# Moving the first norm's gain and shift off VectorE in a two-branch transformer block on one core

## The reference, cut to what matters

```python
# x: 16 x 256 x 128, so 32 tiles of 128 tokens with 128 features each
def _ln(x, g, b, eps=1e-05):
    return (x - mu) / jnp.sqrt(var + eps) * g + b
def _mlp(x, w1, b1, w2, b2):
    return _gelu(x @ w1 + b1) @ w2 + b2
# attention branch, on x already normed once without gain
n = _ln(x, ln_g, ln_b)
W1 = _mlp(n, h1_w1, h1_b1, h1_w2, h1_b2)
W2 = _mlp(n, h2_w1, h2_b1, h2_w2, h2_b2)
W3 = jnp.tril(jnp.einsum('bzn,bsn->bzs', W1, W2))
t = jnp.einsum('bzs,bsm->bzm', W3, n)
t = _ln(_gelu(t), ln_g, ln_b)
out = x + _mlp(_ln(x + t, ln_g, ln_b), fm_w1, fm_b1, fm_w2, fm_b2)
# then a second branch: silu(x w1) * (x w2), two gelu layers of 512 x 512, w3
```

## Time and profile before

| | |
|---|---|
| median of 3 runs | 365.95 us (365.81 to 366.39) |
| span of the profiled execution, first to last instruction | 362.6 us |
| PE, PEld busy | 350.1 us, 289.2 us |
| DVE, ACT, POOL busy | 319.9 us, 305.2 us, 147.2 us |

### The profile page before, as it was taken

One profiled execution on the slowest core, in us unless ns is written; L12 is line 12 of the kernel. 1 busy time (PEld: TensorE's weight loads), 2 busy tenths in 40 slices (PEclk: granted clock), 3 DMA queues, 4 the chain that ended last, 5 costly groups with the idle time before them and its releaser, 6 DMA issues.

```text
span 362.6 us, 6039 instructions
## 1 busy us (share of the span) xinstructions
PE 350.1 (97%) x1788; PEld 289.2 (80%) x1788; DVE 319.9 (88%) x954; ACT 305.2 (84%) x552; POOL 147.2 (41%) x213
## 2 busy tenths in 40 slices
PE   6989999999999999999999999999999999999993
PEld 5867687778888888888888888888888887788992
DVE  5889999999999999889989989998969998886936
ACT  5999999997779979988599888897799569959892
POOL 4168842860546052504750286003920174044411
PEclk9999999999999999999999999999999999999998
DMA  7507020000000000000010001000000001001111
GB/s 233 174 14 245 4 60 1 1 2 1 3 0 0 2 0 2 17 13 2 1 29 3 0 0 33 0 1 2 1 0 2 0 2 31 0 2 29 32 30 33
DMA packets 8804, 9.08 MB, mean 25 GB/s; under 512 B 577, under 2 KB 6722, under 8 KB 8770
## 3 DMA queue, kind: packets, MB, share of 16 engines
q1 hardware_dynamic: 8226, 8.41, 7.7%
q10 hardware_dynamic: 544, 0.26, 0.2%
HBM read 6.57 MB, written 2.10 MB: 24 GB/s over the span
## 4 chain that ended last, share of the span: by engine, by line
PE 67%; ACT 13%; DVE 10%; issue 5%; DMA 2%; POOL 1%; SPq 1%; POOLq 0%; DVEq 0%; ACTq 0%
PE bank L1224 8%; PE bank L1226 8%; PE bank L1240 6%; PE bank L1241 6%; PE bank L1123 4%; PE bank L1104 4%; PE bank L1108 4%; PE bank L1105 4%; PE bank L1120 4%; PE bank L1121 4%; PE bank L1206 4%; PE bank L1209 4%; ACT h_hidden_hi L510 3%; PE bank L1046 2%; ACT bank L515 2%
## 5 line engine op out<-in xcount | busy, mean ns | idle before, releaser
L715 DVE TENSOR_TENSOR ffn_gate_lo<-bank,ffn_gate_hi 128x512 fp32r<-128x512 f32 (+1 forms) x72 | 44.1, 626 | 6.0 <-ACT bank L584 4.9
L510 ACT ACTIVATE h_hidden_hi<-bank,cols 128x512 fp32r<-128x512 f32 x64 | 46.1, 760 | 3.5 <-PE bank L1108 3.2
L515 ACT ACTIVATE bank<-bank,cols 128x512 f32<-128x512 f32 x64 | 45.1, 739 | 0.3
L715 DVE TENSOR_TENSOR h_hidden_lo<-bank,h_hidden_hi 128x512 fp32r<-128x512 f32 x64 | 43.0, 681 | 2.5 <-ACT bank L515 2.5
L584 ACT ACTIVATE bank<-bank,cols 128x512 f32<-128x512 f32 (+1 forms) x72 | 43.7, 620 | 0.7
L1224 PE MATMUL bank<-ffn_gate_hi,ffn_w_hi 128*128 128x512 f32 (+1 forms) x108 | 40.5, 381 | 0.2 <-DVE ffn_gate_lo L715 0.2
L1226 PE MATMUL bank<-ffn_gate_lo,ffn_w_hi 128*128 128x512 f32 (+1 forms) x108 | 39.3, 370 | 0.2 <-DVE ffn_gate_lo L715 0.2
L578 ACT ACTIVATE ffn_h_hi<-bank,cols 128x512 fp32r<-128x512 f32 (+1 forms) x36 | 23.0, 646 | 13.5 <-PE bank L1226 8.3
L578 ACT ACTIVATE ffn_gate_hi<-bank,cols 128x512 fp32r<-128x512 f32 (+1 forms) x36 | 23.2, 647 | 10.6 <-PE bank L1226 8.3
L364 POOL TENSOR_TENSOR XR<-X,ln_x_r 128x512 f32<-128x512 f32 x8 | 8.3, 1042 | 53.6 <-DVE bank L861 53.4
L715 DVE TENSOR_TENSOR ffn_h_lo<-bank,ffn_h_hi 128x512 fp32r<-128x512 f32 (+1 forms) x36 | 22.0, 626 | 8.0 <-ACT bank L584 7.8
(11 more groups left out here) (164 smaller groups left out, 1132.3 us busy)
## 6 DMA issues: line engine op xcount, KB each, us to landing
raw<-ffn_w SPq DMA_DIRECT2D x5, 512.0 KB, 3.9
out<-X SPq DMA_DIRECT2D x7, 256.0 KB, 2.3
raw<-attn_w SPq DMA_DIRECT2D x6, 256.0 KB, 4.9
X<-x SPq DMA_DIRECT2D x3, 256.0 KB, 5.6
raw<-ffn_w SPq DMA_DIRECT2D x1, 256.0 KB, 3.2
X<-x ACTq DMA_DIRECT2D x1, 128.0 KB, 2.5
X<-x SPq DMA_DIRECT2D x1, 128.0 KB, 2.3
out<-X SPq DMA_DIRECT2D x1, 128.0 KB, 1.8
```

What stands on the lines that cost most here:

```text
L510: nc.scalar.activation(dst, bank(f"{L}u{j}", c)[:, :], ACT.Gelu, bias=bias_of(L, j)).then_inc(*hi[L].done(c, j))
L515: nc.scalar.activation(u[:, :], u[:, :], ACT.Gelu, bias=bias_of(L, j)).then_inc(*act2[L].done(c, j))
L715: return nc.vector.tensor_tensor(dst, whole, high.bitcast(f32), ALU.subtract)
```

## The change

The first norm is written without gain and shift by one DVE pass. The up weights of h1 and h2 are scaled by the gain, their biases get the shift times the raw weights, and POOL makes the token form with gain and shift in two passes over NF after PE has transposed it. The bias `fm_b2` is loaded by a DMA with one element per partition. All lists of calls and `TURNS` are laid anew.

```diff
+    UP_PIECES = [PIECE[name] for name in ("h1u", "h2u", "fmu")]
+        h_bias = sb("h_bias", [P, 2 * J])
-        b2_row = M[0:1, 0, :]
@@ SP @@
             attn_piece(2)
-            sp.dma_start(b2_row, rows[2:3, :]).then_inc(b2_in, 16)
             x_piece(1, 1, 2)
             for i in (3, 4, 5):
                 attn_piece(i)
             x_piece(2, 2, 3)
+            sp.dma_start(fm_b2[:, :], rows[2:3, :].rearrange("o d -> d o")).then_inc(b2_in, 16)
             for i in (0, 1):
                 sp.wait_ge(*attn_lo.at(0, 2 * i + 1))
+                if i == 0:
+                    sp.wait_ge(*h_b.at(0))
                 ffn_piece(i)
@@ POOL @@
+            def n_gain(c):
+                if c == 0:
+                    pool.wait_ge(*rows_ready.at(0))
+                pool.wait_ge(*nT.at(c))
+                nc.gpsimd.tensor_tensor(NF[:, :, :], NF[:, :, :], row(R_G), ALU.mult).then_inc(*n_made.done(c, 0))
+
+            def n_shift(c):
+                pool.wait_ge(*n_made.at(c, 0))
+                nc.gpsimd.tensor_tensor(NF[:, :, :], NF[:, :, :], row(R_B), ALU.add).then_inc(*n_made.done(c, 1))
@@ ACT: attn_w_hi @@
-                if i == PIECE["fmu"]:
+                if i in UP_PIECES:
@@ ACT: n_high @@
-                act.wait_ge(*n_v_ready.at(c, T - 1))
+                act.wait_ge(*n_made.at(c, 1))
@@ ACT: bias_of, up_hi (c == 0, j == 0), fm_evict (c == 0) @@
-                return cols[:, C_B1[L] + j:C_B1[L] + j + 1]
+                return h_bias[:, C_B1[L] + j:C_B1[L] + j + 1]
-                        act.wait_ge(cols_in, 16)
+                        act.wait_ge(*h_b_added.at(0))
+                else:
+                    act.wait_ge(b2_in, 16)
@@ DVE: fm_bias_add @@
-                nc.vector.tensor_scalar(fm_b2[:, :], bank("fb", 0)[:, J:J + 1], 1.0, None, ALU.mult)
+            def h_bias_add():
+                dve.wait_ge(*h_b.at(0))
+                nc.vector.tensor_tensor(h_bias[:, :], bank("hb", 0)[:, 0:2 * J], cols[:, 0:2 * J], ALU.add).then_inc(*h_b_added.done(0))
@@ DVE: n_first and n_second give way to @@
-            def n_first(c):
-            def n_second(c):
+            def n_norm(c):
+                if c:
+                    dve.wait_ge(*n_lo.at(c - 1))
+                dve.wait_ge(*x_scale.at(c, 1))
+                for t in range(T):
+                    nc.vector.tensor_scalar(NF[:, t, :], X[:, c * T + t, :], mv("x", c)[:, t, 0:1], x_s[:, t:t + 1],
+                                            ALU.subtract, ALU.mult).then_inc(*n_v_ready.done(c, t))
@@ PE @@
-                pe.wait_ge(b2_in, 16)
-                last = nc.tensor.matmul(bank("fb", 0)[:, J:J + 1], b2_row, ones[0:1, :], start=True, stop=True)
+            def h_bias_product():
+                bank_free("hb", 0)
+                pe.wait_ge(cols_in, 16)
+                for L in ("h1", "h2"):
+                    pe.wait_ge(attn_in[PIECE[f"{L}u"]], 16)
+                    for j in range(J):
+                        w = ATTN[f"{L}u"] + j * P
+                        last = nc.tensor.matmul(bank("hb", 0)[:, C_B1[L] + j:C_B1[L] + j + 1], raw[:, w:w + P], cols[:, C_B:C_B + 1],
+                                                start=True, stop=True)
+                last.then_inc(*h_b.done(0))
@@ the starts of the lists, before and after @@
@@ POOL @@
-            x_s_(0); n_low(0); x_s_(1); x_s_(2); lo_block(0); lo_block(1); x_r(0); xr_scale(0); lo_block(2); xr_b(0)
-            lo_block(3); n_low(1); t_r(0); x_r(1); lo_block(4); lo_block(5); x1_r(0); lo_block(6); lo_block(7); x_s_(3)
+            x_s_(0); n_gain(0); n_shift(0); n_low(0); x_s_(1); n_gain(1); x_r(0); n_shift(1); lo_block(0); lo_block(1)
+            xr_scale(0); x_s_(2); xr_b(0); lo_block(2); lo_block(3); n_low(1); t_r(0); n_gain(2); n_shift(2); lo_block(4)
@@ ACT @@
-            rows_out(); attn_w_hi(0); attn_w_hi(1); n_high(0); nT_high(0); attn_w_hi(2); attn_w_hi(3); attn_w_hi(4)
-            up_hi("h1", 0, 0); up_hi("h1", 1, 0); up_act("h1", 0, 0); up_act("h1", 1, 0); up_hi("h1", 2, 0); up_hi("h2", 0, 0)
+            attn_w_hi(0); rows_out(); attn_w_hi(1); attn_w_hi(2); nT_high(0); attn_w_hi(3); attn_w_hi(4)
+            up_hi("h1", 0, 0); attn_w_hi(5); n_high(0); up_hi("h1", 1, 0); up_act("h1", 0, 0); up_hi("h1", 2, 0)
@@ DVE @@
-            x_st(0); x_ag(0); n_first(0); n_second(0); attn_w_lo(0); attn_w_lo(1); nT_low(0); x_st(1); x_ag(1); n_first(1)
+            x_st(0); x_ag(0); n_norm(0); h_bias_add(); attn_w_lo(0); nT_low(0); x_st(1); gate_constants(); attn_w_lo(1)
+            x_ag(1); attn_w_lo(2); x_st(2); up_lo("h1", 0, 0); attn_w_lo(3); up_lo("h1", 1, 0); n_norm(1)
@@ PE @@
-            fill("rb", 0, 4); make_rows(); fill("nT", 0, 5); n_transpose(0); fill("h1u0", 0, 2); up_mm("h1", 0, 0)
+            fill("rb", 0, 4); make_rows(); fill("nT", 0, 5); h_bias_product(); n_transpose(0); fill("h1u0", 0, 2)
```

More of the change, by code:

```diff
@@ L180, in sandwich_block @@
         ffn_hi, ffn_lo, lo_summed = steps("ffn_hi", FP), steps("ffn_lo", len(F_BLOCKS)), steps("lo_summed", FP)
-        fm_b, fm_b_added = steps("fm_b"), steps("fm_b_added")
+        fm_b, fm_b_added, h_b, h_b_added = (steps(s) for s in ("fm_b", "fm_b_added", "h_b", "h_b_added"))
         gate_consts = steps("gate_consts", 2)
@@ new lines, in _ @@
+            x_r(1); lo_block(5); x1_r(0); x_s_(3); lo_block(6); n_low(2); n_gain(3); lo_block(7); lo_block(8); t_r(1)
+            xr_scale(1); xr_b(1); o_r(0); lo_block(9); x1_r(1); lo_block(10); x_r(2); n_shift(3); y_r(0); y_centre(0)
+            y_scale(0); x_s_(4); o_shift_(0); n_low(3); n_gain(4); n_shift(4); xr_scale(2); o_r(1); x_r(3); xr_b(2)
+            t_r(2); y_r(1); y_centre(1); x1_r(2); n_low(4); y_scale(1); x_s_(5); xr_scale(3); o_shift_(1); n_gain(5)
+            xr_b(3); t_r(3); x_r(4); f_r(0); o_r(2); x1_r(3); y_centre(2); y_r(2); y_scale(2); x_end(0); o_shift_(2)
@@ new lines, in _ @@
+            f_r(1); o_r(3); t_r(4); xr_scale(4); xr_b(4); o_shift_(3); y_r(3); n_shift(5); y_centre(3); x1_r(4)
+            y_scale(3); x_s_(6); n_low(5); n_gain(6); x_r(5); n_shift(6); xr_scale(5); o_r(4); x_end(1); t_r(5)
+            y_centre(4); x_r(6); xr_b(5); y_r(4); y_scale(4); n_low(6); x1_r(5); x_s_(7); o_shift_(4); f_r(2); xr_scale(6)
+            n_gain(7); xr_b(6); o_r(5); o_shift_(5); n_shift(7); x_end(2); f_r(3); y_r(5); y_centre(5); t_r(6); y_scale(5)
+            x_r(7); x1_r(6); n_low(7); xr_scale(7); o_r(6); xr_b(7); x_end(3); t_r(7); y_centre(6); y_r(6); y_scale(6)
@@ new lines, in _ @@
+            up_act("h2", 0, 2); up_act("h1", 2, 2); mT_high(0); up_hi("h2", 1, 2); score_hi(0, 1); up_act("h2", 1, 2)
+            score_hi(1, 1); up_hi("h1", 3, 2); up_hi("fm", 0, 0); up_act("h1", 3, 2); up_act("fm", 0, 0)
+            up_hi("fm", 1, 0); n_high(2); up_act("fm", 1, 0); up_hi("fm", 2, 0); t_act(1); up_act("fm", 2, 0)
+            up_hi("fm", 3, 0); up_hi("h2", 2, 2); up_act("fm", 3, 0); lo_sum(2); lo_sum(3); up_act("h2", 2, 2)
+            fm_evict(0); nT_high(3); up_hi("h2", 3, 2); down_hi("h1", 2); up_act("h2", 3, 2); up_hi("h1", 0, 3)
@@ new lines, in _ @@
+            x_ag(1); attn_w_lo(2); x_st(2); up_lo("h1", 0, 0); attn_w_lo(3); up_lo("h1", 1, 0); n_norm(1)
+            up_lo("h1", 2, 0); up_lo("h2", 0, 0); attn_w_lo(4); up_lo("h1", 3, 0); x_ag(2); up_lo("h2", 1, 0)
+            up_lo("h2", 2, 0); up_lo("h2", 3, 0); nT_low(1); attn_w_lo(5); fm_bias_add(); down_lo("h2", 0)
+            down_lo("h1", 0); score_mask(0, 0); x_st(3); score_mask(1, 0); score_lo(0, 0); score_lo(1, 0)
+            up_lo("h1", 0, 1); up_lo("h1", 1, 1); up_lo("h1", 2, 1); up_lo("h2", 0, 1); t_st(0); t_ag(0); n_norm(2)
```

564 lines of the change are left out of this document (275 added, 289 removed), and 45 rows, old and new, of the table TURNS.

## The result

The changed kernel takes 371.1 us in the median of four runs (369.7 to 373.3), against 365.9 of before in the same comparison: a ratio of 1.0164, 95% interval 1.0123 to 1.0205. It is 1.6% slower, 5.2 us by the two medians and 6.0 by the ratio, where 1.35 us less was forecast.

The account below looks back on a forecast made before the run. PE's work plus its losses at start and end was taken as the bound. Norm -0.9, PE's wait -0.2, ACT +0.6, lists -0.85 gave -1.35 us: 364.6 us against 365.95, range 361.9 to 367.8.

Parts of the forecast that it names:

- So the end is the work of PE plus what PE loses at the start and at the end.: Whole kernel: PE, full from 80 to 280 us, sets the end; its idle time is 2.8 us early, 0.9 late.
- At worst the transposes start 0.4 us later: PE's start: h_bias_product before n_transpose(0) delays the transposes by at most 0.4 us.
- hidden, since ACT waits for weight pieces until 9.88: Start: the bias product's 0.4 us delay costs nothing, as ACT starts the first gelu only at 11.17 us.
- The norm: DVE: n_norm takes 1.37 us per four, at best 0.86, instead of 2.28; saves 0.91 us per chunk, 7.3 in all.
- It fits with no reserve: POOL, 22 to 33 us: n_low(1) ends at about 32.9 us, just when DVE needs it; nothing counted.
- -0.9 us: DVE from 54.00 us: the shorter norm of chunk 3 lies on the path and gains 0.9 us.
- POOL late: Rival, n_norm(2) behind n_low(1) on DVE: POOL's passes don't fit, +2.1 us, 368.0 us; chance 0.20.
- port: Rival, DVE's norm: each four may wait for a POOL pass on the shared port; +0.15 us, 366.1 us; chance 0.06.
- nothing: SP and DMA: the earlier issue, the fm_b2 column load and the later ffn_piece(0) change the time by nothing.
- The lists: All lists: the new order wins a third of the 2.6 us left of PE's idle time, -0.85 us.
- hidden: Rival, full ACT from 10 to 80 us: DVE's saving only lets DVE wait for ACT; 365.9 us, chance 0.17.
- 3.35 us above the span: Frame: the median of the runs lies 3.35 us above the profiled 362.6 us span; the same was added to 361.25.

Follow-up runs that it names:

- a_same: The changed kernel with gate_half and gate_coef packed into one tile, so every operand tile has its address of before; 366.9 us, ratio 1.0050.
- a_again: The changed kernel run once more, unaltered; 370.7 us, ratio 1.0155 to the kernel before.
- b_gap: The kernel before with only an unused 32-byte tile added where h_bias would stand; 368.8 us, ratio 1.0092.
- a_nobias: a_same without the bias product, so the shift is missing in the h1 and h2 biases; 365.2 us, ratio 1.0011.
- a_late: a_ffn with 64-column bias products, h1 half behind the transposes, h2 half before the first h2 up product; 365.4 us, ratio 1.0020.
- a_nopool: a_same without the POOL passes n_gain and n_shift; 366.4 us, ratio 1.0040.
- b_fold: The kernel before, its lists kept, with the fold alone, 64-column bias products and tiles 128 bytes on; 373.2 us, ratio 1.0220.
- a_ffn: a_same with ffn_w_hi(2) moved behind the two score_hi of chunk 0 in ACT's list; 366.2 us, ratio 1.0041.

## Why the prediction was wrong

**The step that failed** is the one on which the sum stands: "So the end is the work of PE plus what PE loses at the start and at the end." The work of PE was taken as given, and its rate had no term. (No run speaks against its being useless to save DVE time between 80 and 280 us; but that does not say that nothing else can move the end there.) The change has an edit that the working passed over, the line `h_bias = sb("h_bias", [P, 2 * J])`. By the place it gives to all tiles behind it, it costs 3.8 us, shown by a_same against a_again and, without the rest of the change, by b_gap (3.4 us).

**The bias product** was a mis-sized term, and its cover was not there. I took 8 instructions for 0.9 us from the earlier trace rows; but those 8 are four products, and here there are eight, so 16 instructions: 1.8 us at 2.4 GHz, 3.4 at 1.2. "At worst the transposes start 0.4 us later" became 3.2 us in the profile where the clock rose late, and 1.0 (7.49 us) in that of a_again. The cover, "hidden, since ACT waits for weight pieces until 9.88", failed in the first, where ACT waited for the transposes themselves (3.18 us at 10.75); in a_again it held, with the first gelu at 10.13 us, earlier than before the change. Over the executions the product costs 1.4 to 1.7 us (a_nobias). The wait that it puts ahead of `attn_w_lo(0)` was named in the working, priced by late weights only, and came true by the product: 2.85 us.

**The norm** was right in kind. Four instructions take 1.12 us (5.83 to 6.95 us), less than the 1.37 taken and more than the bound of 0.86; 340 ns each:

```profile
L789 DVE TENSOR_SCALAR NF<-X,ln_x_mv,ln_x_s 128x128 f32<-128x128 f32 x32 | 8.9, 340 | 1.8 <-POOL ln_x_s L335 1.8
```

That is the duration of each old instruction, and the saving is their halved number, 1.15 us per chunk. In chunk 0 it does not arrive: the one pass needs the scale from POOL from its start, waits 1.43 us for it (a sign of being wrong that the prediction had named) and ends at 6.95 us, where the old pair ended at 7.2. DVE's busy time fell by 5.5 us and not by 7.3 or 9.2, since waits like the two at 12.77 and 25.32 us count as busy, and the scaled weight pieces and the bias add are new; the parts were not measured one by one. The two elements per cycle of the Trainium skill (VectorE: DVE Perf Modes, Mode 2×_2P), weighed in the prediction, show in no row here: 340 ns against the 347 of the old form.

**POOL**'s work came out as counted, 167.0 us against 168 with passes of 1.29 us, its cover only in part. "It fits with no reserve" looked at chunk 1 alone: `n_low(1)` ended at 37.5 us and not at 32.8, and DVE came to `n_norm(2)` at 37.57, without a wait. At chunk 3, at 56.7 us in a_late, the working had only the DVE side, "**-0.9 us**" on the path. There POOL's work ends with DVE's, within 0.03 us, so the chain passes over POOL and a still faster DVE would have had to wait for it; PE has the chain at 74.3 us, and the 0.9 us do not show. What takes them is not shown: without the two passes the time falls by no more than 0.5 us (a_nopool, overlapping intervals). The rival "POOL late" was a loss of 2.1 us at the norm of chunk 2; b_fold shows something like it in the old lists, at another place, the root for M of an earlier chunk. The rival "port": none of the 32 NF instructions met a lock (348 ns at most by the trace), but others did.

**SP and DMA**: "nothing" looked at the first ffn piece alone; the third, sent behind `attn_w_lo(5)`, holds ACT for 1.31 us at 30.41. With ACT's list mended for it, a_ffn is 0.3 us (ratios) to 0.7 us (medians) faster, neither clear of noise.

**The lists**, -0.85: with the addresses of before, the time is 365.2 us with the product left out (a_nobias, ratio 1.0011) and 365.4 with it moved (a_late, 1.0020, 1.0003 to 1.0036), at before's or a little above. That is the number of the rival "hidden". Its reason, an ACT that is as full as before, fits less well: ACT is busy 68.6 of the 70 us from 10 to 80 us in a_late, where it was 69.7. The last PE instruction does end earlier, at 356.6 us in a_late against 357.6 before, with one profile each. But the new order has `f_transpose(7)` behind the last product instead of in front of it, and DVE's part from PE's end to the last store's issue grows from 2.15 to 2.57 us; and in the profile of before the end came some 1.3 us sooner behind that store than in b_gap, whose program is the same. So the forecast gain of 1.35 us, 0.37%, is not there: the interval of a_nobias leaves 0.1% at most.

**The frame** was off as well: the "3.35 us above the span" is not the time around a span. In all runs here the time is 1.7 to 1.9 us above the span of the same execution, so the profiled execution took about 364.3 us by that estimate, some 1.6 below the median: the 3.35 are in part the luck of which execution was profiled.
